# A gated delta-rule recurrence in a software pipeline: two stores moved ahead in ScalarE's queue, and the orders of four queues set anew

## What is computed

```python
q = _causal_dwconv_silu(x @ Wq.T, qcw, qcb).reshape(Bb, Tt, H, DK)
k = _causal_dwconv_silu(x @ Wk.T, kcw, kcb).reshape(Bb, Tt, H, DK) * SCALE
v = _causal_dwconv_silu(x @ Wv.T, vcw, vcb).reshape(Bb, Tt, H, DV)
a = jax.nn.sigmoid(x @ Wa.T + ba).reshape(Bb, Tt, H, DV)
beta = jax.nn.sigmoid(x @ Wb.T + bb)
def step(S, inp):
    qt, kt, vt, at, bt = inp
    err = jnp.einsum('bhij,bhj->bhi', S, kt) - vt
    S = at[..., None] * S - bt[..., None, None] * (err[..., None] * kt[:, :, None, :])
    o = jnp.einsum('bhij,bhj->bhi', S, qt)
    return (S, o)
```

## Time and profile before

| | |
|---|---|
| median of 3 runs | 6990.51 us (6972.95 to 6992.06) |
| time of the profiled execution | 6996.25 us |
| span of its instructions | 6994.4 us |
| busy over the span | PE 5171.4, DVE 5329.3, ACT 3332.5, POOL 3451.6 us |
| mean granted TensorE clock | 0.792 |
| q1 (SyncE's queue) | 500.99 MB, 27.2% of the DMA engines' span |
| q10 (ScalarE's queue) | 185.09 MB, 11.0% |

### The profile page before, as it was taken

How to read it: one execution, slowest core, us unless ns; L and a number is a source line. 1 busy time by engine, 2 the same in 40 slices (tenths; PEclk the granted TensorE clock), 3 DMA queues, 4 the chain that set the end, 5 groups by cost and what they waited for, 6 DMA issues and landing times. The chain is left out here.

```text
span 6994.4 us, 177868 instructions
## 1 busy us (share of the span) xinstructions
PE 5171.4 (74%) x59191; PEld 3349.9 (48%) x59191; DVE 5329.3 (76%) x15729; ACT 3332.5 (48%) x7298; POOL 3451.6 (49%) x4488
## 2 busy tenths in 40 slices
PE   3677767777777777777777727888888888888888
PEld 2455555555555555555555513444444444344343
DVE  4888988888888888888888856666666666666665
ACT  4445555455554455555455513444444444444444
POOL 1777877777777777777777751111111111111110
PEclk9777777777777777777777758888888888888888
DMA  4555555555555555555555531111111111111111
GB/s 163 136 131 136 139 141 144 133 134 134 139 142 138 131 134 139 141 139 138 125 141 141 140 82 46 46 45 45 45 46 46 46 47 45 45 45 45 45 46 34
DMA packets 1195973, 695.80 MB, mean 99 GB/s; under 512 B 1054936, under 2 KB 1106808, under 8 KB 1193593
## 3 DMA queue, kind: packets, MB, share of 16 engines
q1 hardware_dynamic: 888044, 500.99, 27.2%
q10 hardware_dynamic: 307200, 185.09, 11.0%
HBM read 371.99 MB, written 313.95 MB: 98 GB/s over the span
## 5 line engine op out<-in xcount | busy, mean ns | idle before, releaser
L1855 DVE TENSOR_REDUCE nmax<-w_bank 128x1 f32<-128x512 f32 x1024 | 642.8, 684 | 406.2 <-PE w_bank L1437 401.5
L941 DVE SCALAR_TENSOR_TENSOR p_bank<-y,conv_w,p_bank 128x128 f32<-128x128 f32 x3072 | 819.7, 350 | 117.1 <-ACT p_bank L753 82.3
L535 POOL TENSOR_TENSOR qp<-qp,ab 128x512 f32<-128x512 f32 (+7 forms) x1024 | 871.7, 851 | 75.2
L540 POOL TENSOR_TENSOR qp<-qp,pt 128x512 f32<-128x512 f32 (+7 forms) x1024 | 839.4, 820 | 80.3
L677 PE MATMUL p_bank<-xnT,wqkv 128*128 128x128 f32 x4096 | 699.3, 341 | 67.0 <-ACT xnT L838 56.3
L677 PEld LDWEIGHTS p_bank<-xnT,wqkv 128*128 128x128 f32 x4096 | 652.5, 250 | 144.7 <-issue 144.7
L1392 POOL TENSOR_TENSOR ot<-ot,ln_w 128x1024 f32<-128x1024 f32 x64 | 151.0, 2359 | 1136.0 <-ACT ot L1694 1136.0
L537 POOL TENSOR_TENSOR pt<-qp,vb 128x512 f32<-128x512 f32 (+7 forms) x1024 | 696.1, 680 | 10.9 <-DVE vb L998 10.9
L1397 POOL TENSOR_TENSOR x1b<-x,bias 128x256 f32<-128x256 f32 x64 | 46.4, 726 | 1172.4 <-DVE bst L1951 1172.4
L1668 ACT ACTIVATE pt<-e_bank 128x1024 f32<-128x1024 f32 x512 | 514.0, 1021 | 181.1 <-PE e_bank L1467 179.7
L612 PE MATMUL d_bank<-st 64*32 64x80 f32 x16384 | 442.0, 267 | 109.8 <-issue 70.3
(11 more groups left out here) (234 smaller groups left out, 11326.5 us busy)
## 6 DMA issues: line engine op xcount, KB each, us to landing
prod_dram<-prod ACTq DMA_DIRECT2D x64, 1280.0 KB, 9.0
kp<-prod_dram SPq DMA_DIRECT2D x64, 640.0 KB, 5.6
qp<-prod_dram SPq DMA_DIRECT2D x64, 640.0 KB, 7.2
a_dram<-at ACTq DMA_DIRECT2D x64, 512.0 KB
ab<-a_dram SPq DMA_DIRECT2D x64, 512.0 KB, 5.9
v_dram<-vt ACTq DMA_DIRECT2D x64, 512.0 KB
vb<-v_dram SPq DMA_DIRECT2D x64, 512.0 KB, 4.6
vt<-e_dram SPq DMA_DIRECT2D x64, 512.0 KB
```

The costliest lines, as they stand in the source:

```text
L535: link(nc.gpsimd.tensor_tensor(q, q, ab[:, g, r:r + 1, :].to_broadcast([128, w, DV]), ALU.mult), 1)
L540: link(nc.gpsimd.tensor_tensor(q, q, pt2[:, 0:w], ALU.add))
L941: nc.vector.scalar_tensor_tensor(out=zz, in0=y[:, j % Y_BANKS, i, :, tap:tap + C], scalar=conv_w[:, m, tap:tap + 1], in1=zz, op0=ALU.mult, ...
L1855: nc.vector.tensor_reduce(nmax[:, n:n + 1], bank[:], AX.X, ALU.max, negate=True).then_inc(freed, 1)
```

## The change

No instruction is added, taken away or altered. What changes is the order in which each engine's slot lists its work.

- ScalarE: `store_gates` and `store_betas` stood behind `products` and the first `evict` of step s+2. Now they stand behind `silu(4)`, ahead of `silu(5)`, `values` and `products`. `silu(2)` and `evict(5)` come after `betas`; `evict(3)` comes ahead of `silu(1)`; `evict(s+2, 1)` comes ahead of `key_rows`.
- VectorE: `conv(8)` moves from ahead of the first half to behind the first two decays; `conv(9)` stands between the decays (4, 5) and (6, 7); the later `conv` steps stand between other pairs of `state`.
- TensorE: `project(5)` moves from the front of the slot to just ahead of `update(0)`; `project(s+2, 0)` moves from between the updates to behind the products; `gate` and `betas` stand ahead of all but the first two spreads.
- SyncE: the output's store comes first, and x is loaded next to it. The decays' store and ab's load come between xe and xk; nb's load ahead of vb's; qp's load ahead of the updates' store.

```diff
@@ sync @@
+                if valid(lo - 1, hi - 1):
+                    sp.wait_ge(pool_chain, POOL_OPS * s)
+                    ... o_dram store, ahead of the loads of xd
...
-                    sp.dma_start(ab[:, o], a_dram[o].rearrange("t b h i -> (b h) t i")).then_inc(ab_in[o], 16)
+                    load_x(n + 2, g)
                 if valid(lo, hi):
                     sp.wait_ge(solve_chain, SOLVE_OPS * s + FIRST_HALF_OPS)
...
                     sp.dma_start(xe[:], e_dram[g].rearrange("t b h i -> b t (h i)")).then_inc(xe_in[g], 16)
-                    sp.wait_ge(*dma_of(x_wr, n, g, 0, 32))
-                    held(sp, sp_passed)
-                    sp.dma_start(xk[:], x_dram[g].rearrange("t b h i -> (b h) t i")).then_inc(xk_in[g], 16)
                 if updates(lo, hi):
...
                 if valid(lo + 1, hi + 1):
+                    sp.dma_start(ab[:, o], a_dram[o].rearrange("t b h i -> (b h) t i")).then_inc(ab_in[o], 16)
+                if valid(lo, hi):
+                    sp.wait_ge(*dma_of(x_wr, n, g, 0, 32))
+                    held(sp, sp_passed)
+                    sp.dma_start(xk[:], x_dram[g].rearrange("t b h i -> (b h) t i")).then_inc(xk_in[g], 16)
...
@@ tensor @@
-                if front:
-                    project(s + 1, 1 - g, 3)
                 if state:
                     spread(*before, (0, 1))
                 if front:
-                    project(s + 1, 1 - g, 4)
-                    project(s + 1, 1 - g, 5)
+                    project(s + 1, 1 - g, 3)
                 if ahead:
                     gate(s + 2, g, 0)
+                if front:
+                    project(s + 1, 1 - g, 4)
+                if ahead:
                     gate(s + 2, g, 1)
+                    betas(s + 2, g)
                 if state:
                     spread(*before, (2, 3))
                     spread(*before, (4, 5))
-                if ahead:
-                    betas(s + 2, g)
+                    spread(*before, (6, 7))
+                if front:
+                    project(s + 1, 1 - g, 5)
                 if state:
-                    spread(*before, (6, 7))
                     update(*before, (0,))
                 if valid(lo, hi):
                     cross(s, n, g)
...
@@ scalar @@
                 if front:
                     silu(s + 1, 1 - g, 4)
+                if ahead:
+                    store_gates(s + 2, n + 1, g)
+                    store_betas(s + 2, n + 1, g)
+                if front:
                     silu(s + 1, 1 - g, 5)
                     place_keys(s + 1, 1 - g)
                     values(s + 1, n + g, 1 - g)
                     products(s + 1, n + g, 1 - g)
                 if ahead:
                     evict(s + 2, g, 0)
-                    store_gates(s + 2, n + 1, g)
-                    store_betas(s + 2, n + 1, g)
+                    evict(s + 2, g, 1)
                 if front:
                     key_rows(s + 1, 1 - g)
@@ vector @@
-                    for k in range(0, 9):
+                    for k in range(0, 8):
                         conv(s + 1, k)
                 if now:
                     half(s, n, g, 0)
+                if update:
+                    decay(s - 1, 1 - g, (0, 1))
+                if front:
+                    conv(s + 1, 8)
+                if update:
+                    decay(s - 1, 1 - g, (2, 3))
+                    decay(s - 1, 1 - g, (4, 5))
...
                 if update:
                     state(s - 1, 1 - g, (0, 1))
                 if front:
-                    for k in range(12, 17):
+                    for k in range(14, 16):
                         conv(s + 1, k)
                 if update:
                     state(s - 1, 1 - g, (2, 3))
+                if front:
+                    for k in range(16, 18):
+                        conv(s + 1, k)
+                if update:
                     state(s - 1, 1 - g, (4, 5))
-                if front:
-                    conv(s + 1, 17)
-                if update:
                     state(s - 1, 1 - g, (6, 7))
```

More of the change, by code:

```diff
@@ L380, in slot @@
                                      upd_dram[o][b].rearrange("h t i -> t h i")).then_inc(xd_in[o], 16)
-                if valid(lo - 1, hi - 1):
-                    sp.wait_ge(pool_chain, POOL_OPS * s)
-                    held(sp, sp_passed)
[L384 to L388, removed]
+                if valid(lo + 4, hi + 4):
+                    if not isinstance(s, int) or s + 2 >= 0:
+                        sp.wait_ge(f_filled, front1_use(s + 2) + 1)
                         held(sp, sp_passed)
-                    sp.wait_ge(*dma_of(a_wr, n, g, 1))
-                    held(sp, sp_passed)
-                    sp.dma_start(ab[:, o], a_dram[o].rearrange("t b h i -> (b h) t i")).then_inc(ab_in[o], 16)
+                    load_x(n + 2, g)
                 if valid(lo, hi):
@@ L707, in slot @@
                     update(*before, (1,))
-                if ahead:
-                    project(s + 2, g, 0)
-                if state:
-                    update(*before, (2,))
                 if front:
@@ L714, in slot @@
                 if state:
+                    update(*before, (2,))
                     update(*before, (3,))
@@ L719, in slot @@
                     front2(s + 1, n + g, 1 - g, (2,))
+                if ahead:
+                    project(s + 2, g, 0)
+                if front:
                     front2(s + 1, n + g, 1 - g, (3,))
@@ L873, in slot @@
                 if front:
+                    evict(s + 1, 1 - g, 3)
                     silu(s + 1, 1 - g, 1)
-                    silu(s + 1, 1 - g, 2)
-                    evict(s + 1, 1 - g, 3)
                     evict(s + 1, 1 - g, 4)
@@ L879, in slot @@
                     gates(s + 2, n + 1, g)
-                if front:
-                    evict(s + 1, 1 - g, 5)
-                if ahead:
                     betas(s + 2, n + 1, g)
                 if front:
+                    silu(s + 1, 1 - g, 2)
+                    evict(s + 1, 1 - g, 5)
                     silu(s + 1, 1 - g, 3)
@@ L900, in slot @@
                 if ahead:
-                    evict(s + 2, g, 1)
                     evict(s + 2, g, 2)
@@ L1034, in slot @@
                 if update:
-                    decay(s - 1, 1 - g, (0, 1))
-                    decay(s - 1, 1 - g, (2, 3))
-                    decay(s - 1, 1 - g, (4, 5))
                     decay(s - 1, 1 - g, (6, 7))
                 if front:
-                    for k in range(10, 12):
+                    for k in range(10, 14):
                         conv(s + 1, k)
```

32 lines of the change are left out of this document (17 added, 15 removed).

## The result

The changed kernel takes 7165.68 us (7160.6 to 7166.29), the kernel before in the same session 6991.28 us. The ratio is 1.0251, with a 95% interval of 1.0229 to 1.0273: 174 us slower, where the forecast said 76 slower, and outside the forecast's own range (7020 to 7140), though inside the wide one. The profiled execution has a span of 7164.4 us and a mean granted clock of 0.777 instead of 0.792. In the experiments they shift again by a line or two; the names of the tiles stay.

A forecast was written before the change was run, and what follows sets the result against it. VectorE was busiest, but a round trip through xk's load set the pace. Terms +0.7, +1.9, -1.4 gave +1.2 us a step, +76 us over 63 steps, 7066 us; range 7020 to 7140, wide range 6915 to 7220.

The forecast's parts named there:

- the wide one: The prediction's wider range for the changed kernel's time, 6915 to 7220 us.
- Term (4): ScalarE's DMA queue: the gates' 512 KB store ahead of xk's load delays xk by +1.9 us a step.
- the lower bound of 0: Gates' store and xk's load share the DMA engines without loss, so xk is delayed by 0 us.
- Term (1) and (2): ScalarE's gates' store issues sooner, about 0.35 us for VectorE; conv 8 leaves xk's stretch, 1.06 us: together -1.4 us a step.
- Term (3): TensorE: project(5) ahead of update(0) makes cross start 1 to 1.9 us later, taken as +0.7 us a step.
- both of its cases: TensorE's update(0) ends at U + 11.8 if the clock stays low, near 10.9 if it rises behind the projection.
- up to 0.5 us: SyncE's queue: price on the round trip if decays' stores and ab's load, taken as free, made xe suffer.
- v's store joined: Rival: v's store overlaps xk's load, +3.1 us or more on top, 7260 us; chance 0.14 shared with ScalarE held.
- xk isn't delayed: Faster rival: the gates' store doesn't delay xk, 6946 us, or 6902 us with the clock up early; chance 0.29.
- the gates' store would hold ScalarE at its new place: Rival: ScalarE is held 4 us ahead of silu(5), a step longer by 2 us or so; chance 0.02.

The follow-up runs named there:

- after: The changed kernel with all four engines' new orders, against the kernel before: 7165.68 us, ratio 1.0251.
- The loops of four slots: Four slots in each loop turn instead of two: changed kernel 7112.2 us, changed kernel with the stores back 7047.87 us, kernel before 7016.1 us.
- the stores back: Changed kernel with the gates' and betas' stores returned behind evict(s+2, 0), other orders as changed: 7160.75 us, ratio 1.0241 against the kernel before.

## Why the prediction was right or wrong

**The sign and its mechanism: right.** Term (4), the gates' store in xk's way, was forecast at +1.9 us and measured at +2.11 in after and +2.12 in the kernel that moves nothing but the stores. The Trainium skill (DMA: Bandwidth & Descriptors, section "Queues, rings and completion order") says that a DMA engine takes turns between queues by the packet. By that rule xk's 256-byte pieces fall behind beside 4096-byte ones; the page itself doesn't draw this, and the trace agrees: 6.16 us to the last packet instead of 3.88. xk's first packet starts as early as before (1.10 us after the issue, before 1.02), so the load runs beside the store and not behind it. The first step of the trace of before was the right row to lean on, and the lower bound of 0 fell. That the size fits so well is partly luck. The store's first packet is 1.7 us ahead of xk's issue, not the 1.1 estimated, so by the forecast's own working 2.1 us of it were left and the delay 1.4 us. The sharing slows the store too (5.9 us from its first to its last packet in after, 4.7 in the kernel before), which the working had at nothing.

**Term (1) and (2): right in sum.** -1.4 was forecast for the conv stretch, -1.45 measured; L852 takes 0.59 us, and VectorE's wait for `evict(1)` is gone. The 4 us that ScalarE gained beyond that were worth nothing on VectorE's path, as the sum had it.

**Term (3), `cross` later: the step that failed, mis-sized at +0.7 us where xk's issue moved by +1.49.** Two things were in it. (a) The forecast took off about half of `cross`'s delay for a clock that rises behind the projection. The projection ran at the lower level, as in both of its cases, and the clock then did rise in most steps: `cross` takes 2.67 us over the fifty steps instead of 3.62 and is under 2.5 in 27 of them. But from its start to xk's issue pass 9.12 us instead of 9.45, so only 0.33 of the 0.95 us is passed on, for 5.1 of the 9.12 us pass behind the issue of the second store of x, until both have landed. In odd steps, which the back edge spares, `cross` starts 1.12 us later (10.01 to 11.13), only 0.07 is passed on, and xk's issue is late by 1.05 us (19.26 to 20.31). (b) Even steps are late by 1.93 us (19.58 to 21.51), 0.44 us more over the mean, because TensorE comes late out of the back edge. The forecast had read a single slot, and the word "issue" ahead of L621 stood in no step of it. The loops of four slots show it. Behind these two stands xe. The forecast let the decays' stores and ab's load pass at no cost, and named the price of a mistake: "up to 0.5 us". SyncE's order alone makes `cross` 0.75 us later and the kernel 0.55% slower. In after TensorE is later still and covers this; with three quarters of `project(5)` away `cross` comes only 0.8 us earlier, and then xe holds it.

**The first half, +0.33 us: at nothing in the sum.** Its last product (L1022, here L1023) takes 1.29 us instead of 1.01 on average, which is 0.28 of it; the median of all 64 goes from 951 to 1520 ns. The traces show what it waits for. The row of 2175.34 above, with GpSimd's beside it:

```profile
2175.12 1.26 POOL L540 TENSOR_TENSOR qp<-qp,pt 128x512 f32<-128x512 f32 x1
2175.34 1.59 DVE L1023 TENSOR_TENSOR eb<-vb,eb 128x512 f32<-128x512 f32 x1
```

In all of the fifty steps of after the product ends 0.55 to 0.57 us after the end of the GpSimd instruction that was running when it started (here 2176.93 after 2176.38), and in 49 of the fifty before 0.55 to 0.69. What was left of that instruction is 0.75 us on average instead of 0.45. So the product waits for GpSimd, and the new orders moved the two against each other. No run tests it by moving GpSimd alone.

**The size as a whole.** Measured less forecast is 2.61 - 1.2 = 1.41 us a step: 0.79 from term (3), 0.33 from the first half, 0.21 from term (4), 0.13 from the second half, -0.05 from the conv stretch. Times 63 that is 89 of the 98 us by which the forecast was short; some 6 of the rest lie outside the recurrence's steps (164 of the span's 170 us are in them).

**The rivals.** v's store joined, but only at the end: xk is used at U + 27.69 and v's store goes out at 2137.08, U + 24.76. On average 26 of its 128 pieces start before xk's last packet. That costs nothing that can be seen: with the stores alone moved, xk's last packet comes after 6.07 us in the 30 steps where v's pieces join and after 6.28 in the 20 where they don't. xk was there 6.55 us after its issue, not 9.14. "xk isn't delayed" fell. That the gates' store would hold ScalarE at its new place fell as well (0.59 us).

**Why the parts don't add.** The stores alone cost 1.56%, the engines' orders 2.17%, SyncE's order 0.55%: 4.28% in sum, and all together 2.51%. The orders of engines and SyncE together, without the stores, cost 2.41%, so the stores on top of them add 0.10%, which is within the noise. I read it so: the step waits for whichever is later, and each of the two had room behind the other: the slow transfer of xk makes the step longer and gives TensorE time to catch up (xk's issue at U + 20.91), and with the stores back xk is quick but TensorE is not there (U + 23.29). So undoing the part with the proven mechanism won nothing.

## What to carry to other kernels

Where a store is moved, look for the load that it will share DMA engines with, not only for the issuer that it frees: here 512 KB in 4096-byte rows, on half of the DMA engines by the share of 0.47, cost a load in 256-byte rows 2.1 us, more than the 4 us of freed issuer were worth. What is said to be off the critical path needs its distance in us, for every engine and at the loop's back edge too; a second path of almost the same length makes undoing a proven fault win nothing. An average is read from many steps: the one step printed here has `cross` at the lower clock throughout, and most have not. Test the parts one by one from both ends, added to the kernel before and taken from the kernel after: only the two together show such a pair, and they also found the one edit worth keeping.

## What the runs showed of the hardware that was not expected

- TensorE's time at the loop's back edge is not fixed. Between 1000 and 3900 us it idles 4.2 us there on average in the kernel before, 5.6 in after and 7.1 with the stores back. A load of 16 KB of instructions appears in the trace in each. Its packets start 0.75 us behind the loop's branch in the kernel before (median 0.41), 2.9 in after and 4.4 with the stores back, and in the latter two TensorE goes on 2.9 us after they start. So there the idle time is about the lateness of this load plus 2.9 us. Why it starts later is open. Half as many back edges moved the ratio by -1.42%, -0.63% and +0.42%, by where TensorE stood.
- In the step shown TensorE's clock stayed at its lower level through a projection, an update and all of `cross`: the row of 2118 to 2124 has PE busy for 6.00 us of 6.00 at a granted clock of 0.50, and `cross` runs until 2127.45 at 3.64 us, after the spreads with their pauses. With the stores back the same three ran in one go too, from 2130.15, and there `cross` took 1.99 us: by then the higher level had come.
- A VectorE product of two tensors (L1022) took 0.69 to 1.79 us by where GpSimd stood: it ended about 0.55 us after the GpSimd instruction that was running when it started.
- Whether an issue is cheap depends on what lies in its queue. The gates' store took 0.59 us to issue behind the two stores of x (256 KB each) and 4.5 us (mean) behind the products' store (1280 KB); the betas' store took 2.48 us behind two stores of 512 KB. Behind the products' store the issue ends at about the same time wherever it begins: 6.16 us after the products' store is issued in the kernel before, where it begins at 1.69, and 6.22 with `evict(s+2, 1)` first, where it begins at 4.30 (means). The Trainium skill (DMA: Bandwidth & Descriptors, section "Issuing engines are not separate DMA queues") calls this time "usually small relative to the DMA itself"; in the kernel before it is as long as the transfer, whose packets take 4.7 us.
